# Two of three layer norms moved to ScalarE, a shorter output norm, and router weights written by GpSimd

## The chip, the cores and the metric
The kernel runs on one core of a Trainium2 chip. The metric is the time of one execution in microseconds. The core's engines work side by side, each through its own list of instructions: TensorE (PE in the rows, its weight loads PEld), VectorE (DVE), ScalarE (ACT), GpSimd (POOL) and SyncE (SP), which issues DMAs. They meet only at semaphores: an instruction may wait until a semaphore has reached a value, and everything behind it on its engine waits with it.

## What is computed
One decoder layer on x (8 batches x 512 tokens x 256 features, fp32), in three steps, each on a normalized copy of x and added to x:
```
x = x + attn(layernorm(x))       # gated slot attention: 4 heads, 64 slots, a recurrence over the tokens
x = x + xattn(layernorm(x))      # 16 heads against 64 context rows, softmax with 1 added to the denominator
x = x + moe(layernorm(x))        # 8 experts, top 2 of 8, 1280 places per expert, silu gate
layernorm(x) = (x - mean) / sqrt(var + 1e-5)
```
The slot attention ends in an output norm for each head, `o = o * rsqrt(mean(o*o) + 1e-5) * g_norm_w`, where o is a softmax-weighted sum, so that o is an unnormalized sum u divided by the softmax's denominator s. The router takes the two largest of 8 logits, gives them the weights 1/(1+e) and e/(1+e) with e = exp(second - first), and a token keeps its place with an expert only while that expert has taken fewer than 1280.

## The kernel before
The first stage goes over 32 chunks of 128 tokens, four to a batch. The second goes over the experts in 40 groups of 256 places.

Each engine's list for the chunk stage is written by hand as a `step` (PE L1516, DVE L1190, ACT L779, POOL L610): a fixed order of named pieces of work, each with a lag. `run(2, x_scores)` in step s means the piece for chunk s-2. So a step holds the slot attention of chunk s (lag 0) and its end for chunk s-1, the cross attention's start for s-1 and its middle for s-2, its end and the router's norm for s-3, and the routing for s-4. The first two batches and the last lagging steps are unrolled; the six batches between run in a loop, whose turn falls on the first chunk of a batch.

What the change and the prediction touch:
- **Norms.** `statistics` (L902) makes mean and variance on DVE in x_mv (r_mv, f_mv) and var+eps; `power` (L543) on POOL raises that to -0.5 (x_rstd, r_rstd, f_rstd); `norm` (L913) on DVE applies (x - mean) * rstd, giving f_xn, x_xn and r_xn. The norms are f (first), x (before the cross attention, lag 1) and r (before the router, lag 3). r_norm writes the row twice, 512 columns, into r_xn, whose rows are sent to the experts; each row has two more columns, the token's number and its weight.
- **Order on DVE** at the end of a step: residual2, start_states, r_statistics, residual1, x_statistics, causal_scores, x_norm, r_norm, slot_logits, gate_probs.
- **Order on POOL:** f_power, values, head_power, send_rows, keys (only a batch's first chunk, at lag 1: two 128x512 products, k_bd), r_power, hidden_keys (hid, from the mask), x_power. `hold` (L539) is a 128x1 add into idle_g that only takes time.
- **Order on ACT:** ..., o_columns, x_exp, ks_columns (k_z, s_z), e_columns (e_t, the copy of the cross attention's transposed exponentials), x_columns, softmax_exp (b_e), r_columns, p_columns, x_queries, squares.
- **Order on PE:** ..., scores, e_columns, logits, x_columns (transposes of x_xn and hid), values (the product of e_t with v_bd), r_columns, p_columns (transposes of b_p), x_queries, mix, sum_states, read_out.
- **Output norm:** DVE sums squares (b_ss), multiplies twice by the softmax's reciprocal (b_t1, b_t2), scales and adds eps (b_ms), POOL raises to -0.5 (b_rms), DVE multiplies by the reciprocal (b_w) and applies it (b_o). Between them DVE runs x_maximum (sc_m).
- **Routing:** top_two (L1136) ends in `both`, which PE counts; places (L1160) makes the place numbers, the weights r_p and r_p*r_e, writes them into r_xn, and ends in `send`, on which POOL's send_rows (L597) waits before it issues two indirect DMAs.

Of the kernel before, what the change touches and what calls it, by code (L numbers as in the profile page):

```python
# [70 lines left out]
ROUTE_STEPS = 11  # L71
# [5 lines left out]
def decoder_layer(nc, x, qpos, kpos, mask, ctx_t, wq, wk, wv, wf, gnorm, wo,  # L77
# [5 lines left out]
    with ctx:  # L83
# [9 lines left out]
        neg_half = sb("neg_half", [P, 4])  # L93
        idle_v, idle_g = sb("idle_v", [P, 1]), sb("idle_g", [P, 3])
# [24 lines left out]
        def part1(name, shape, dt=F32):  # L119
# [49 lines left out]
        lg_m, b_sum, b_rec, b_ss, b_t1, b_t2, b_ms, b_rms, b_w = (  # L169
            part1(t, [P, H]) for t in ("lg_m", "b_sum", "b_rec", "b_ss", "b_t1", "b_t2", "b_ms", "b_rms", "b_w"))  # L170
# [7 lines left out]
        x_st, x_mv, x_var, x_rstd = (part1(t, [P, w]) for t, w in (("x_st", 6), ("x_mv", 2), ("x_var", 1), ("x_rstd", 1)))  # L178
        x_xn = part1("x_xn", [P, D])
# [23 lines left out]
        base = part1("base", [P, 2])  # L203
# [41 lines left out]
        def sems(names):  # L245
# [9 lines left out]
        logits_mm, lg_ok, lgm_ok, lgd_ok, be_ok, bsum_ok, brec_ok, bp_ok, p_mm, p_ok, mix_mm, mix_ok = sems(  # L255
            "logits_mm lg_ok lgm_ok lgd_ok be_ok bsum_ok brec_ok bp_ok p_mm p_ok mix_mm mix_ok")
        read_mm, sq_ok, rms_step, ms_ok, rms_ok, bw_ok, bo_ok, o_mm, o_ok, y_mm, x1_ok = sems(
            "read_mm sq_ok rms_step ms_ok rms_ok bw_ok bo_ok o_mm o_ok y_mm x1_ok")
# [82 lines left out]
        CONSTS = 19 + XH  # L341
# [138 lines left out]
        def _(pool):  # L480
# [10 lines left out]
            pool.memset(neg_half[:, :], -0.5).then_inc(consts_step, 1)  # L491
            pool.memset(taken[:, :], 0.0).then_inc(consts_step, 1)
# [4 lines left out]
            pool.wait_ge(consts_step, 7 + XH)  # L497
# [13 lines left out]
            pool.wait_ge(consts_step, 13 + XH)  # L511
# [11 lines left out]
            pool.wait_ge(consts_step, 18 + XH)  # L523
# [123 lines left out]
        def _(act):  # L647
# [47 lines left out]

            def e_columns(n, c, b):
# [63 lines left out]
            def squares(n, c, b):  # L760
                act.wait_ge(read_mm, n + 1)
                if later(n, 1):
                    act.wait_ge(rms_step, 3 * n)
# [9 lines left out]
            def router_exp(n, c, b):  # L773
                act.wait_ge(gap_ok, n + 1)
                if later(n, 1):
                    act.wait_ge(slots_ok, n)
                act.activation(r_e[:, :], gap[:, :], ACT.Exp).then_inc(re_ok, 1)

            def step(run):  # L779
# [9 lines left out]
                run(0, ks_columns)  # L789
                run(2, e_columns)  # L790
# [55 lines left out]
        def _(dve):  # L846
# [176 lines left out]
            def softmax_sum(n, c, b):  # L1023
# [3 lines left out]
                dve.reciprocal(b_rec[:, :], b_sum[:, :]).then_inc(brec_ok, 1)  # L1027
# [8 lines left out]
            def head_squares(n, c, b):  # L1036

                dve.wait_ge(sq_ok, n + 1)
                dve.tensor_reduce(b_ss[:, :], b_sq[:, :, :], AX.X, ALU.add).then_inc(rms_step, 1)
                dve.wait_ge(rms_step, 3 * n + 1)  # L1040
                dve.wait_ge(brec_ok, n + 1)
                dve.tensor_tensor(b_t1[:, :], b_ss[:, :], b_rec[:, :], ALU.mult).then_inc(rms_step, 1)

            def head_squares2(n, c, b):
                dve.wait_ge(rms_step, 3 * n + 2)
                dve.tensor_tensor(b_t2[:, :], b_t1[:, :], b_rec[:, :], ALU.mult).then_inc(rms_step, 1)
                dve.wait_ge(rms_step, 3 * n + 3)
                if later(n, 1):
                    dve.wait_ge(rms_ok, n)
                dve.tensor_scalar(b_ms[:, :], b_t2[:, :], 1.0 / M, EPS, ALU.mult, ALU.add).then_inc(ms_ok, 1)  # L1050

# [569 lines left out]
```

## Time and profile before
| | |
|---|---|
| runs | 1523.87, 1531.29, 1534.08 us (median 1531.29) |
| the profiled execution | 1525.26 us, its span 1523.5 us |
| PE busy | 1406.5 us (92%) |
| PE weight loads | 1257.8 us (83%) |
| DVE busy | 952.5 us (63%) |
| ACT busy | 657.0 us (43%) |
| POOL busy | 351.9 us (23%) |
| mean granted clock of PE | 0.967 |

A busy share is the part of the span in which an engine executed instructions; matmuls are pipelined and their ends are modelled, so a busy PE isn't PE at its peak. The shares are averages over two stages of different kinds. In a timeline row stand the start, the busy time (both us), the engine, the line, the operation and its tiles; in square brackets, where there is one, the idle time of the engine just before it and what ended that. Rows of one line are merged where they follow each other.

### The profile page before, as it was taken

Reading aid. Unit: us, or ns where it says so; the run is one execution under the profiler, and the core shown is the slowest. Engines: PE = TensorE matmul, PEld = TensorE weight load, DVE = VectorE, ACT = ScalarE, POOL = GpSimd, SP = SyncE. Lnnn points to the kernel's source line nnn. Section 1 sums busy time; section 2 is a strip of 40 time slices with the busy share of each in tenths; the row PEclk is TensorE's granted clock in tenths of the full one; section 3 lists DMA queues with packets and bytes.
Section 4 is the critical chain, followed back from the end, with each engine's and each line's share of the span. In section 5 each row is a group of like instructions: output and inputs, shape, how many; then the busy total and the mean of one; then the engine's idle time right before and its main releaser. Section 6 shows DMA issues by size and latency. Waiting matters only on the chain. (4 is left out here: it accounts for less than half of the span.)

```text
span 1523.5 us, 31744 instructions
## 1 busy us (share of the span) xinstructions
PE 1406.5 (92%) x10457; PEld 1257.8 (83%) x10457; DVE 952.5 (63%) x3165; ACT 657.0 (43%) x1658; POOL 351.9 (23%) x523
## 2 busy tenths in 40 slices
PE   5699999999999999999975999999999999999995
PEld 3577777777777777777754999999999999999995
DVE  4367787787787787777744555556554555556442
ACT  1244554454554554454413444334443444344331
POOL 3112322232231322322212112122111212122122
PEclk8799999999999999999966999999999999999998
DMA  9300010010100100000006133142414133142111
GB/s 278 102 12 17 31 31 16 31 30 15 30 30 15 30 30 16 30 30 15 22 21 210 26 81 63 29 117 34 115 29 113 31 74 78 29 122 33 29 22 22
DMA packets 67288, 79.62 MB, mean 52 GB/s; under 512 B 11091, under 2 KB 60724, under 8 KB 67155
## 3 DMA queue, kind: packets, MB, share of 16 engines
q1 hardware_dynamic: 52562, 59.09, 12.8%
q0 software_dynamic: 14592, 18.91, 7.6%
q8 instruction: 65, 1.06, 0.3%
q14 instruction: 69, 0.56, 0.1%
HBM read 44.04 MB, written 33.96 MB: 51 GB/s over the span
## 5 line engine op out<-in xcount | busy, mean ns | idle before, releaser
L830 ACT ACTIVATE h_a<-banks 128x256 f32<-128x256 f32 x320 | 122.5, 383 | 359.2 <-PE banks L1309 359.2
L1241 DVE TENSOR_TENSOR h_f<-banks,h_a 128x256 f32<-128x256 f32 x320 | 135.7, 424 | 158.6 <-ACT h_a L830 149.0
L541 POOL TENSOR_TENSOR idle_g<-half 128x1 f32<-128x1 f32 x144 | 29.8, 207 | 709.5 <-DVE y_s L1260 409.6
L1309 PE MATMUL banks<-xe_t_hi,w_even_hi 128*128 128x256 f32 x640 | 180.2, 282 | 0.9 <-DVE h_f L1241 0.9
L1309 PE MATMUL banks<-xe_t_hi,w_odd_hi 128*128 128x256 f32 x640 | 179.5, 280 | 0.0
L1309 PE MATMUL banks<-xe_t_lo,w_even_hi 128*128 128x256 f32 x640 | 178.3, 279 | 0.0
L1309 PE MATMUL banks<-xe_t_hi,w_even_lo 128*128 128x256 f32 x640 | 178.2, 279 | 0.0
L1309 PE MATMUL banks<-xe_t_lo,w_odd_hi 128*128 128x256 f32 x640 | 177.9, 278 | 0.0
L1309 PE MATMUL banks<-xe_t_hi,w_odd_lo 128*128 128x256 f32 x640 | 177.8, 278 | 0.0
L817 ACT ACTIVATE h_t_hi<-h_f 128x256 fp32r<-128x256 f32 x320 | 131.8, 412 | 32.6 <-DVE h_f L1241 32.2
L1248 DVE TENSOR_TENSOR h_t_lo<-h_f,h_t_hi 128x256 fp32r<-128x256 f32 x320 | 133.8, 418 | 6.1 <-ACT h_t_hi L817 4.3
L635 POOL DMA_INDIRECT out_dram<-y_s,token x80 | 124.7, 1559 | 27.0 <-issue 19.9
L1309 PEld LDWEIGHTS banks<-xe_t_hi,w_even_hi 128*128 128x128 f32 x640 | 121.1, 189 | 1.1 <-DVE h_f L1241 1.1
L1309 PEld LDWEIGHTS banks<-xe_t_lo,w_even_hi 128*128 128x128 f32 x640 | 121.4, 190 | 0.0
L1309 PEld LDWEIGHTS banks<-xe_t_lo,w_odd_hi 128*128 128x128 f32 x640 | 121.0, 189 | 0.0
L1309 PEld LDWEIGHTS banks<-xe_t_hi,w_even_lo 128*128 128x128 f32 x640 | 120.8, 189 | 0.0
L1309 PEld LDWEIGHTS banks<-xe_t_hi,w_odd_hi 128*128 128x128 f32 x640 | 120.3, 188 | 0.0
L1309 PEld LDWEIGHTS banks<-xe_t_hi,w_odd_lo 128*128 128x128 f32 x640 | 120.1, 188 | 0.0
L1309 PE MATMUL banks<-w_in,f_xnt 128*128 128x512 f32 (+1 forms) x256 | 99.8, 513 | 1.9 <-ACT f_xnt L655 1.9
L1258 DVE CAST token<-about 128x1 uint32<-128x1 f32 x80 | 8.6, 149 | 134.0 <-PE banks L1309 134.0
L1309 PE MATMUL banks<-w_odd_hi,h_t_hi 128*128 128x256 f32 x320 | 88.8, 278 | 0.0
L1309 PE MATMUL banks<-w_even_hi,h_t_hi 128*128 128x256 f32 x320 | 88.8, 278 | 0.0
(240 smaller groups left out, 3669.3 us busy)
## 6 DMA issues: line engine op xcount, KB each, us to landing
raw<-in_w SPq DMA_DIRECT2D x24, 1024.0 KB, 8.3
expert_rows<-empty SPq DMA_DIRECT2D x4, 2580.0 KB, 22.4
xe<-expert_rows SPq DMA_DIRECT2D x40, 258.0 KB, 2.9
xin<-in_x SPq DMA_DIRECT2D x32, 128.0 KB, 2.2
out_dram<-x SPq DMA_DIRECT2D x32, 128.0 KB, 1.8
out_dram<-y_s,token POOLq DMA_INDIRECT x80, 3.8
mask_i<-in_mask SPq DMA_DIRECT2D x32, 32.0 KB, 1.8
expert_rows<-r_xn,send POOLq DMA_INDIRECT x64, 3.2
```

What stands on the lines that cost most here:

```text
L541: return pool.tensor_tensor(idle_g[:, i:i + 1], half[:, 0:1], half[:, 0:1], ALU.add)
L635: pool.indirect_dma_start(out=out, out_offset=bass.IndirectOffsetOnAxis(ap=token[par][a][:, :], axis=0), in_=y_s[:, par, a, :], in_offset= ...
L817: act.activation(h_t[0][:, par, f, :], h_f[:, f % 2, :], ACT.Copy).then_inc(h_hi_ok, 1)
L830: act.activation(h_a[:, f % 2, :], bank[2 + f % 4][:, 0:GS], ACT.Silu).then_inc(silu_ok, 1)
L1241: dve.tensor_tensor(h_f[:, f % 2, :], bank[2 + f % 4][:, GS:2 * GS], h_a[:, f % 2, :], ALU.mult)\
L1248: dve.tensor_tensor(h_t[1][:, par, f, :], h_f[:, f % 2, :], h_t[0][:, par, f, :], ALU.subtract)\
L1258: dve.tensor_copy(token[par][a][:, :], about[:, par, a, 0:1])
L1309: last = pe.matmul(dst, lhs, rhs, start=(i == 0), stop=(i == len(pairs) - 1))
```

## The change
Three edits, all in the chunk stage:
1. x_norm and r_norm are applied by ACT as scale*x + bias with scale rstd and bias -mean*rstd. POOL makes the bias (x_shift, r_shift) right after the power. On ACT the two stand between ks_columns and e_columns. f_norm stays on DVE.
2. The output norm's weight is one power: with s the softmax's sum, (ss/64 + eps*s*s)^-0.5 is the weight. The reciprocal, b_t1, b_t2 and b_w's product go; one scalar_tensor_tensor on s (b_floor) comes.
3. The router's weights and the token's number are written into r_xn by POOL in send_rows, the reciprocal as a power of -1. DVE's places gets shorter, hot is made by one instruction, and DVE's last routing step waits for the sends of two chunks before.

```
@@ gpsimd @@
+            def shift(n, mv, rstd, to, rstded, shifted, i):
+                pool.wait_ge(rstded, n + 1)
+                hold(i)
+                pool.tensor_scalar(to[:, :], mv[:, 0:1], rstd[:, 0:1], -1.0, ALU.mult, ALU.mult).then_inc(shifted, 1)
             def x_power(n, c, b):
                 power(n, x_var, x_rstd, x_vared, x_rstded, x_normed)
+                shift(n, x_mv, x_rstd, x_shift, x_rstded, x_shifted, 3)
             def r_power(n, c, b):
                 power(n, r_var, r_rstd, r_vared, r_rstded, r_normed)
+                shift(n, r_mv, r_rstd, r_shift, r_rstded, r_shifted, 4)
             def head_power(n, c, b):
-                power(n, b_ms, b_rms, ms_ok, rms_ok, bw_ok)
+                power(n, b_ms, b_w, ms_ok, bw_ok, bo_ok)
...
+                pool.wait_ge(re_ok, n + 1)
+                hold(0)
+                pool.tensor_scalar(r_den[:, :], r_e[:, :], 1.0, 1e-12, ALU.add, ALU.add).then_inc(send_step, 1)
+                pool.wait_ge(send_step, n * SEND_STEPS + 1)
+                pool.tensor_tensor(r_p[:, :], r_den[:, :], neg_one[:, :], ALU.pow).then_inc(send_step, 1)
+                pool.tensor_copy(r_xn[:, par, :, D:D + 1],
+                                 token_no[:, bass.ds(n, 1)].rearrange("p (a b) -> p a b", b=1).to_broadcast([P, 2, 1]))
+                pool.wait_ge(send_step, n * SEND_STEPS + 2)
+                pool.tensor_tensor(r_xn[:, par, 1, D + 1:ROW], r_p[:, :], r_e[:, :], ALU.mult)
+                pool.tensor_copy(r_xn[:, par, 0, D + 1:ROW], r_p[:, :]).then_inc(send_step, 1)
                 pool.wait_ge(slots_ok, n + 1)
-                hold(0)
+                pool.wait_ge(r_normed, n + 1)
+                pool.wait_ge(send_step, n * SEND_STEPS + SEND_STEPS)
+                hold(5)
@@ scalar @@
+            def x_norm(n, c, b):
+                act.wait_ge(x_shifted, n + 1)
...
+                act.activation(x_xn[:, :], x1[:, c % 2, :], ACT.Identity, bias=x_shift[:, 0:1], scale=x_rstd[:, 0:1])\
+                   .then_inc(x_normed, 1)
+            def r_norm(n, c, b):
...
+                act.wait_ge(r_shifted, n + 1)
+                act.activation(r_xn[:, c % 2, :, 0:D],
+                               x2[:, c % 2, :].rearrange("p (a d) -> p a d", a=1).to_broadcast([P, 2, D]),
+                               ACT.Identity, bias=r_shift[:, 0:1], scale=r_rstd[:, 0:1]).then_inc(r_normed, 1)
...
                 run(0, ks_columns)
+                run(3, r_norm)
+                run(1, x_norm)
                 run(2, e_columns)
@@ vector @@
-                dve.reciprocal(b_rec[:, :], b_sum[:, :]).then_inc(brec_ok, 1)
+                dve.scalar_tensor_tensor(out=b_floor[:, :], in0=b_sum[:, :], scalar=EPS, in1=b_sum[:, :],
+                                         op0=ALU.mult, op1=ALU.mult).then_inc(floor_ok, 1)
...
-                dve.tensor_tensor(b_t1[:, :], b_ss[:, :], b_rec[:, :], ALU.mult).then_inc(rms_step, 1)
...
-                dve.tensor_tensor(b_t2[:, :], b_t1[:, :], b_rec[:, :], ALU.mult).then_inc(rms_step, 1)
...
-                dve.tensor_scalar(b_ms[:, :], b_t2[:, :], 1.0 / M, EPS, ALU.mult, ALU.add).then_inc(ms_ok, 1)
+                dve.scalar_tensor_tensor(out=b_ms[:, :], in0=b_ss[:, :], scalar=1.0 / M, in1=b_floor[:, :],
+                                         op0=ALU.mult, op1=ALU.add).then_inc(ms_ok, 1)
...
-                dve.tensor_tensor(b_w[:, :], b_rms[:, :], b_rec[:, :], ALU.mult).then_inc(bw_ok, 1)
...
-                for k in range(2):
-                    dve.tensor_scalar(hot[:, k, :], expert_no[:, :], top_f[:, k:k + 1], None, ALU.is_equal)\
+                dve.tensor_tensor(hot[:, :, :], expert_no[:, :].rearrange("p (a e) -> p a e", a=1).to_broadcast([P, 2, E]),
+                                  top_f[:, :].rearrange("p (k a) -> p k a", a=1).to_broadcast([P, 2, E]), ALU.is_equal)\
...
-                dve.tensor_scalar(base[:, :], top_f[:, :], float(CAP), None, ALU.mult).then_inc(route_step, 1)
-                dve.wait_ge(re_ok, n + 1)
-                dve.tensor_scalar(r_den[:, :], r_e[:, :], 1.0, 1e-12, ALU.add, ALU.add).then_inc(route_step, 1)
...
-                dve.reciprocal(r_p[:, :], r_den[:, :]).then_inc(route_step, 1)
...
-                dve.tensor_tensor(slot_f[:, :], pos[:, :], base[:, :], ALU.add).then_inc(route_step, 1)
...
-                dve.tensor_copy(r_xn[:, c % 2, 0, D + 1:ROW], r_p[:, :])
-                dve.tensor_tensor(r_xn[:, c % 2, 1, D + 1:ROW], r_p[:, :], r_e[:, :], ALU.mult)
+                dve.scalar_tensor_tensor(out=slot_f[:, :], in0=top_f[:, :], scalar=float(CAP), in1=pos[:, :],
+                                         op0=ALU.mult, op1=ALU.add).then_inc(route_step, 1)
...
-                run(1, x_norm)
-                run(3, r_norm)
```

## Rows read from the trace of the kernel before
**Rows 1.** Busy time by stretch: PE, PEld, DVE, ACT, POOL, clock, DMA share, GB/s.
```profile
400.00:500.00 100.00, 92.96 (x607) 74.34 (x606) 79.46 (x316) 52.88 (x134) 28.20 (x45) 1.00 0.09 26
...
820.00:1500.00 680.00, 675.86 (x5867) 675.09 (x5866) 362.79 (x914) 283.89 (x723) 134.34 (x152) 1.00 0.28 63
```
**Rows 2.** Waits, 100 to 740 us: who waited for whom, us in total, times, longest.
```profile
PE banks L1309 <- DVE both L1158: 5.7, 5, 1.2
...
PE banks L1309 <- DVE g_s L946: 5.0, 24, 0.2
PE banks L1303 <- DVE f_xn L915: 4.0, 5, 0.9
...
PE banks L1303 <- DVE b_p L1020: 1.7, 7, 0.2
```
**Rows 3.** Timeline of a batch's third step: start, us, engine, line, operation, idle before.
```profile
447.49 0.19 ACT L777 ACTIVATE r_e<-gap 128x1 f32<-128x1 f32 x1
...
449.45 0.19 POOL L541 TENSOR_TENSOR idle_g<-half 128x1 f32<-128x1 f32 x1 [4.97 <-DVE send L1188]
...
452.88 1.16 PE L1309 MATMUL banks<-q_t,k_z 128*128 128x128 f32 x8 [0.33 <-issue]
...
453.43 0.56 POOL L548 TENSOR_TENSOR r_rstd<-r_var,neg_half 128x1 f32<-128x1 f32 x1 [0.84 <-DVE r_var L911]
...
453.98 0.18 POOL L541 TENSOR_TENSOR idle_g<-half 128x1 f32<-128x1 f32 x1
454.13 0.44 POOL L594 TENSOR_SCALAR hid<-mask_i 128x64 f32<-128x64 int32 x1
...
454.75 0.57 POOL L548 TENSOR_TENSOR x_rstd<-x_var,neg_half 128x1 f32<-128x1 f32 x1 [0.18 <-DVE x_var L911]
455.01 1.08 ACT L701 ACTIVATE e_t<-banks 128x512 f32<-128x512 f32 x2 [1.39 <-PE banks L1477]
...
455.43 0.41 DVE L915 TENSOR_SCALAR x_xn<-x,x_mv,x_rstd 128x256 f32<-128x256 f32 x1 [0.21 <-POOL x_rstd L548]
...
456.44 0.39 PE L1303 MATMUL banks<-ident,x_xn 128*128 128x128 f32 x2
...
456.66 1.86 PEld L1309 LDWEIGHTS banks<-v_bd,e_t 128*128 128x128 f32 x16
...
459.01 0.20 PEld L1303 LDWEIGHTS banks<-ident,b_p 128*128 128x128 f32 x2 [0.35 <-DVE b_p L1020]
```
**Rows 4.** Groups of POOL's instructions, 0 to 60 us: count, busy us, mean ns.
```profile
L530 POOL TENSOR_SCALAR sl<-slopes 128x16 f32<-128x16 f32 x1 | 1.1, 1107 | 0.1
```
**Rows 5.** Groups of ACT's instructions, 0 to 740 us.
```profile
L716 ACT ACTIVATE f_e<-f_abs 128x256 f32<-128x256 f32 x31 | 12.9, 417 | 0.0
...
L648 ACT ACT_TABLE_LOAD x1 | 1.3, 1283 | 0.8 <-PEq L1612 0.8
```
**Rows 6.** Timeline of a batch's second step, with k_bd.
```profile
429.82 2.05 POOL L570 TENSOR_TENSOR k_bd<-k_all,diag 128x512 f32<-128x512 f32 x2
...
434.36 1.86 PEld L1309 LDWEIGHTS banks<-v_bd,e_t 128*128 128x128 f32 x16
...
436.84 0.44 PE L1303 MATMUL banks<-ident,b_p 128*128 128x128 f32 x2 [0.24 <-DVE b_p L1020]
```
**Rows 7.** Timeline of a batch's first step, in two batches.
```profile
402.99 0.20 ACT L777 ACTIVATE r_e<-gap 128x1 f32<-128x1 f32 x1 [0.78 <-DVE gap L1147]
...
403.88 0.18 PE L1309 MATMUL banks<-both,before 128*128 128x8 bf16 x1 [1.15 <-DVE both L1158]
...
409.78 0.58 POOL L548 TENSOR_TENSOR x_rstd<-x_var,neg_half 128x1 f32<-128x1 f32 x1
...
411.72 1.86 PEld L1309 LDWEIGHTS banks<-v_bd,e_t 128*128 128x128 f32 x16
...
489.51 0.16 DVE L1042 TENSOR_TENSOR b_t<-b_ss,b_rec 128x4 f32<-128x4 f32 x1
489.70 0.16 DVE L1046 TENSOR_TENSOR b_t<-b_t,b_rec 128x4 f32<-128x4 f32 x1
```

More of the change, by code:

```diff
@@ L70 @@
 SPARE = B * T
-ROUTE_STEPS = 11
+ROUTE_STEPS = 7
+SEND_STEPS = 3
 PIECES = 6
@@ L168, in decoder_layer @@
         lg, lg_d, b_e = (part1(t, [P, H, M]) for t in ("lg", "lg_d", "b_e"))
-        lg_m, b_sum, b_rec, b_ss, b_t1, b_t2, b_ms, b_rms, b_w = (
-            part1(t, [P, H]) for t in ("lg_m", "b_sum", "b_rec", "b_ss", "b_t1", "b_t2", "b_ms", "b_rms", "b_w"))
+        lg_m, b_sum, b_floor, b_ss, b_ms, b_w = (
+            part1(t, [P, H]) for t in ("lg_m", "b_sum", "b_floor", "b_ss", "b_ms", "b_w"))
         b_p = part1("b_p", [P, D])
@@ L178, in decoder_layer @@
         x_st, x_mv, x_var, x_rstd = (part1(t, [P, w]) for t, w in (("x_st", 6), ("x_mv", 2), ("x_var", 1), ("x_rstd", 1)))
+        x_shift, r_shift = part1("x_shift", [P, 1]), part1("r_shift", [P, 1])
         x_xn = part1("x_xn", [P, D])
@@ L339, in is_last @@
             return isinstance(n, int) and n == last
-        CONSTS = 19 + XH
+        CONSTS = 20 + XH
         W_LOADS = 11 + B
@@ L694, in ks_columns @@
                     last.then_inc(done, 1)
+            def x_norm(n, c, b):
+                act.wait_ge(x_shifted, n + 1)
+                if later(n, 1):
+                    act.wait_ge(x_cols_mm, n)
+                act.activation(x_xn[:, :], x1[:, c % 2, :], ACT.Identity, bias=x_shift[:, 0:1], scale=x_rstd[:, 0:1])\
+                   .then_inc(x_normed, 1)
+            def r_norm(n, c, b):
+                if later(n, 2):
+                    for k in range(2):
+                        act.wait_ge(sent[2 * (c % 2) + k], (n - c % 2) * 8)
+                    act.wait_ge(r_cols_mm, n - 1)
+                act.wait_ge(r_shifted, n + 1)
+                act.activation(r_xn[:, c % 2, :, 0:D],
+                               x2[:, c % 2, :].rearrange("p (a d) -> p a d", a=1).to_broadcast([P, 2, D]),
+                               ACT.Identity, bias=r_shift[:, 0:1], scale=r_rstd[:, 0:1]).then_inc(r_normed, 1)
             def e_columns(n, c, b):
@@ L1071, in x_statistics @@
                 statistics(n, x1[:, c % 2, :], x_st, x_mv, x_var, x_stats, x_vared, x_rstded)
-            def x_norm(n, c, b):
-                if later(n, 1):
-                    dve.wait_ge(x_cols_mm, n)
-                norm(n, x1[:, c % 2, :], x_xn[:, :], x_mv, x_rstd, x_rstded, x_normed)
             def x_maximum(n, c, b):
@@ L1118, in r_statistics @@
                 statistics(n, x2[:, c % 2, :], r_st, r_mv, r_var, r_stats, r_vared, r_rstded)
-            def sent_before(n, c):
-                if later(n, 2):
-                    for k in range(2):
-                        dve.wait_ge(sent[2 * (c % 2) + k], (n - c % 2) * 8)
-            def r_norm(n, c, b):
-                sent_before(n, c)
-                if later(n, 2):
-                    dve.wait_ge(r_cols_mm, n - 1)
-                norm(n, x2[:, c % 2, :].rearrange("p (a d) -> p a d", a=1).to_broadcast([P, 2, D]),
-                     r_xn[:, c % 2, :, 0:D], r_mv, r_rstd, r_rstded, r_normed)
-                dve.tensor_copy(r_xn[:, c % 2, :, D:D + 1],
-                                token_no[:, bass.ds(n, 1)].rearrange("p (a b) -> p a b", b=1).to_broadcast([P, 2, 1]))
             def top_two(n, c, b):
@@ L1151, in top_two @@
                 dve.wait_ge(route_step, n * ROUTE_STEPS + 2)
[L1152 to L1155 removed]
+                dve.tensor_tensor(hot[:, :, :], expert_no[:, :].rearrange("p (a e) -> p a e", a=1).to_broadcast([P, 2, E]),
+                                  top_f[:, :].rearrange("p (k a) -> p k a", a=1).to_broadcast([P, 2, E]), ALU.is_equal)\
+                   .then_inc(route_step, 1)
+                dve.wait_ge(route_step, n * ROUTE_STEPS + 3)
                 if later(n, 1):
@@ L1194, in step @@
                 run(1, head_squares)
-                run(1, head_squares2)
                 run(2, x_maximum)
-                run(1, head_weights)
                 run(1, head_outputs)
```

53 lines of the change are left out of this document (23 added, 30 removed).

## The prediction
> **What bounds the kernel now.** The stretches by engine come first [rows 1]. The stretch from 400 to 500 us stands for the stage of the 32 chunks: TensorE (PE) is busy 93 us of 100 there, VectorE (DVE) 79, ScalarE (ACT) 53, GpSimd (POOL) 28. From 820 us the experts run, PE busy 676 of 680 us; the change touches nothing there. So whatever the change is worth, it is worth it in the chunk stage, and only where PE waits.
>
> The waits of that stage come next [rows 2]. PE's idle time that ends on a DVE result is small: 5.7 us before the counts, 5.0 before the gate sums, 4.0 before the transposes of f_xn, 1.7 before those of b_p, together 16.4 us of 640. That is the most that a lighter DVE can give back, and DVE's 79% is no bound.
>
> Then the timeline of one ordinary chunk, row by row [rows 3]. PE takes its work in the written order: logits, transposes of x_xn (456.44), values (456.77). The values product reads e_t, which ACT begins at 455.01 and ends at 456.09, before PE comes to it. The transposes need x_xn, which DVE ends at 455.84 (455.43 and 0.41), also before. Both have about 0.5 us of slack and no more. In front of x_xn stands POOL's chain: r_rstd 453.43, hold, hid 454.13, x_rstd 454.75 to 455.32, nearly without a gap. POOL is mostly idle over a chunk, but not in these two microseconds.
>
> **The change, part by part.** Times are those of the chunk in [rows 3] unless said otherwise.
>
> *Shift chain on POOL.* The two norms become scale and bias on ACT, so POOL must also make -mean*rstd. Behind r_rstd come a wait for it, a hold and a 128x1 tensor_scalar; the same behind x_rstd. A hold passes in 0.15 (453.98 to 454.13). No row shows a warm 128x1 tensor_scalar: from below it is bounded by the 128x1 add, 0.19 busy; from above by hid, 128x64, 0.44; far above lies the setup's first one, 1.1 us [rows 4]. I take 0.30, between the two warm ones, and 0.07 for a wait on POOL itself (between 0 and 0.15). So each shift adds 0.52. r_rstd ends at 453.99, r_shift at 454.51, hid (0.15 and 0.44) at 455.10, x_rstd (0.57) at 455.67, x_shift at 456.19.
>
> *Norms on ACT.* They stand behind ks_columns and ahead of e_columns. ACT's 256 columns from SBUF take 0.417 [rows 5]; DVE took 0.41 for x_xn. r_norm (512 columns, at most twice that) waits for r_shift and runs from 454.6 to 455.4, covered. x_norm waits for x_shift: 456.29 to 456.71. Behind it on ACT waits e_columns, whose input has been ready since 455.01; it now runs from about 456.67 to 457.75 (1.08 in all). So PE comes to x_xn's transposes 0.3 late, and to the values product at 457.8 instead of 456.7 (weight load): **1.1 us later**. What follows on PE (the b_p transposes, which waited 0.35 for their weights, [rows 3], some 0.1 of it on PE) is then ready, which gives back 0.1. Net 1.0. All later work of the chunk hangs on PE's order, so none of this is made up.
>
> The Trainium skill ("ScalarE: Activation LUTs", Rules for kernel authors) says to put multiply and add on VectorE, which it gives as up to about 3 times faster than ScalarE in bf16. The rows show 0.41 against 0.417 for this fp32 size, so the trace does not bear it out. By the rule's factor x_norm would take 1.2 us and each chunk 0.8 us more, 26 us in all.
>
> *Router weights on POOL.* DVE sheds base, r_den, r_p, two writes to r_xn and the token column; POOL gains a hold, a tensor_scalar, a power of one column (0.57, as x_rstd), two copies and a product (0.2 each, as the hold), and a second hold. They can start when r_e is there (447.68) and end by 449.4. The first hold before the sends stood at 449.45, released by DVE's send, which comes some 0.2 earlier now: the sends move by nothing. With 0.44 per tensor_scalar and 0.3 per small one they would be 0.55 late. What hides that is POOL's wait of 0.84 ahead of r_rstd [rows 3], except where k_bd is built.
>
> *Chunk with keys.* In one chunk of four POOL builds k_bd (2.05) between the sends and r_rstd [rows 6], from 429.82 to 431.87, so there is no gap for the shifts to fall into. With the steps above r_rstd ends at 432.44, r_shift at 432.96, hid at 433.55, x_rstd at 434.12, x_shift at 434.64, x_norm at 435.15, e_t at 436.2, and values starts 1.8 later than its 434.36 (weight load). PE's wait of 0.24 for b_p goes. Net 1.6.
>
> *First chunk of a batch.* The loop's turn makes DVE late, and PE waits 1.15 for both [rows 7]. Here the lighter DVE counts: two b_t steps, b_w and one hot go ahead of it, at 0.19 each (from 489.51 to 489.70 for the first), so both comes 0.75 earlier, r_e some 0.5 earlier (ACT waited 0.78 for gap), and the sends 0.7 earlier. POOL ran its chain here without a gap, so x_rstd moves from 409.78 to 409.6 (0.7 earlier, 0.52 of r_shift later), x_shift ends at 410.7, x_norm at 411.2, e_t at 412.25; values starts 0.6 later than its 411.72, less the 0.1 of b_p. Net 0.5.
>
> *Output norm by one power.* The reciprocal becomes a scalar_tensor_tensor of the same size; b_t twice and b_w leave DVE. Elsewhere than in the first chunk of a batch, sc_m behind them waits for PE and starts when it did, so 0.2 is gained at b_w and 0.17 at hot; g_s comes 0.24 earlier, and PE's wait of 0.2 before it closes. But the scores wait 0.33 behind k_z on ACT [rows 3], which hangs on qk_e, not on g_s, so the 0.2 reappears there. I cost it at nothing; if k_z were no wall it would give 0.2 x 24 = 5 us, the share of the g_s waits in [rows 2].
>
> **Sum.** A batch: 0.5 + 1.6 + 1.0 + 1.0 = 4.1 us, times 8 batches = 33 us. The profiled execution took 1525.3 us (span 1523.5); 1558 after. The three runs' median, 1531.3, lies 6 above it, so I put the median at 1561. With 0.19 for every tensor_scalar: about 3.0 a batch, 24 us, 1549. With 0.44 and slow copies: 0.8 + 2.4 + 1.3 + 1.3 = 5.8, 46 us, 1571 (median 1577).
>
> **Rivals.**
> (a) *The lighter DVE wins (faster).* Place: the counts and g_s waits. It decides if x_norm ends before about 455.55, so that e_t is not late. Then the 16.4 us of [rows 2] are open, at best 1515 by the median. Against it: x_rstd alone ended at 455.32 and two holds, two shifts and x_norm come on top, at least 1.2 us even with the add's price. 4%.
> (b) *The slip is absorbed.* PE comes late to values, but PE's records may hide idle time behind it (the ends of matmuls are modelled), or the delay may shrink later waits, such as the 0.33 a chunk before the scores; 18 us or more of the 33 would go, and 1546 or less would be left. For: these waits exist. Against: each of them hangs on work that starts after PE's own. 9%, of which 1% ends above the 15 us.
> (c) *POOL's tensor_scalar costs 1.1 us warm, as the setup's did* [rows 4]. Then POOL is late for the sends by 0.9 and each shift adds 1.3: some 2.6 to 4 us a chunk, 1610 to 1650. Against: hid, the same instruction on 64 columns, takes 0.44. 7%.
> (d) *Identity needs another activation table.* ACT loads a table once, 1.3 us [rows 5]; a switch before r_norm and one back before the softmax's exponential would add 2.6 us a chunk to an ACT that is now on the path: 33 + 83 us, 1647. For it: no Identity stands in the trace. Against: Copy, Square and Abs run beside Exp and Ln without a load. 2%.
> The Trainium skill ("ScalarE: Activation LUTs", Table sets) says that identity is in every set; by that rule (d) is void.
> (e) *The edits do nothing to the path* (all of it beside PE's work): 1531. That would need e_columns ahead of x_norm, which the diff excludes; it shares the chance of (b).
>
> **Numbers.** The forecast holds 78%. Predicted 1561. The range reaches from 1542 (below the cheapest prices, into (b)) to 1590 (above the dear ones, towards (c)). A measurement of this kernel can tell about 1% (15 us) from no change: faster 0.04, same 0.08, slower 0.88.
>
> **What would show it.** In the changed trace: ACT idle before x_xn with POOL x_shift as releaser, some 1 us in each chunk; ACT's idle time before e_t (1.39 in [rows 3]) gone; e_t beginning right behind x_xn; PE waiting for x_xn and e_t, 0.8 to 1.8 us a chunk together; DVE's share falling with PE no faster; PE's wait for both shrinking below 0.5. The forecast is wrong if PE does not wait for e_t, if the chunk stage lengthens by under 15 us, or if POOL's x_shift ends within 0.5 us of the old x_rstd.

## The result and the profile after
| | before | after |
|---|---|---|
| median | 1527.6 us (4 runs, 1523.87 to 1534.08) | 1646.57 us (4 runs, 1645.34 to 1650.31) |
| profiled execution, span | 1525.26, 1523.5 us | 1650.31, 1648.6 us |
| mean granted clock of PE | 0.967 | 0.919 |

After takes 1.0778 times as long [1.0729, 1.0827]: 119 us more, where 33 were forecast. (The four runs of before include the three of the table ahead of the prediction, whose median was 1531.29.)

The page of after: engines, and the granted clock in 40 slices (9 is 90% or more).
```profile
PE 1494.9 (91%) x10457; PEld 1342.5 (81%) x10457; DVE 899.7 (55%) x2781; ACT 693.4 (42%) x1722; POOL 427.5 (26%) x844
...
PEclk8799898999898998989887599999999999999998
```
Busy time by stretch of after, columns as in [rows 1]: the chunk stage, a pause and what follows it, the experts.
```profile
140.00:700.00 560.00, 509.09 (x2989) 418.42 (x2989) 341.94 (x1204) 267.73 (x660) 184.19 (x426) 0.90 0.07 23
...
485.00:489.70 4.70, 2.35 (x18) 1.76 (x16) 1.84 (x4) 2.53 (x5) 2.62 (x9) 1.00 0.03 7
489.70:499.00 9.30, 9.28 (x54) 9.28 (x55) 3.12 (x11) 1.83 (x6) 0.17 (x1) 0.63 0.00 0
...
940.00:1620.00 680.00, 677.81 (x5815) 677.62 (x5814) 360.72 (x908) 280.63 (x719) 134.80 (x152) 0.99 0.28 63
```
The same of before: the chunk stage, and the stretch behind a values product's start.
```profile
140.00:700.00 560.00, 529.07 (x3466) 424.87 (x3465) 435.63 (x1693) 281.16 (x715) 149.84 (x238) 1.00 0.08 25
...
456.50:466.00 9.50, 9.38 (x72) 7.90 (x72) 6.54 (x22) 2.60 (x8) 0.96 (x2) 1.00 0.00 1
```
The experts run as in [rows 1]. In the chunk stage DVE falls as meant, from 436 to 342 us of 560, and PE does less too: 2989 matmuls where there were 3466. The two rows in the middle hold the part that [rows 1] to [rows 7] do not show. PE is busy for 2.35 of 4.7 us and is granted 1.00; then it is busy for 9.28 of 9.30 us and is granted 0.63, a mixture of its two levels, 1.2 and 2.4 GHz. 54 matmuls pass there in 9.3 us, where before passed 72 in 9.5.

PE's waits of after, 100 to 860 us (who waited for whom, us in total, times, longest), to be held against [rows 2].
```profile
PE banks L1305 <- ACT x_xn L723: 22.1, 29, 1.7
PE banks L1311 <- ACT e_t L742: 16.9, 28, 0.8
...
PE banks L1305 <- ACT decay L788: 6.2, 24, 0.7
PE banks L1311 <- DVE both L1171: 4.2, 5, 0.9
...
PE banks L1311 <- DVE g_s L989: 1.1, 6, 0.2
```
The forecast waits are there, in every chunk: 39.0 us in about 28, of which 1.6 us (for x_xn, in the steps with k_bd) stood in before too. What the lighter DVE gives back is small. The wait for both falls from 5.7 to 4.2 us. The wait for g_s falls from 5.0 to 1.1, but the one for decay, which ACT makes from the product of g_s and which PE reads next but one, grows from 1.1 to 6.2: the 0.2 us a chunk is not gained, it is waited for one piece later. ACT's longer list is not the cause: norms_only below has that list and waits 1.1 us for decay from 100 to 740 us, and no_norms_pad has the short list and waits 5.1 us from 140 to 700. The timeline of a batch's second step, with k_bd, of after ([rows 6] of before):
```profile
485.83 0.26 POOL L560 TENSOR_SCALAR r_shift<-r_mv,r_rstd 128x1 f32<-128x1 f32 x1
...
486.74 0.56 POOL L551 TENSOR_TENSOR x_rstd<-x_var,neg_half 128x1 f32<-128x1 f32 x1
...
487.66 0.27 POOL L560 TENSOR_SCALAR x_shift<-x_mv,x_rstd 128x1 f32<-128x1 f32 x1
487.96 0.60 ACT L723 ACTIVATE x_xn<-x,x_shift,x_rstd 128x256 f32<-128x256 f32 x1 [0.94 <-POOL x_shift L560]
488.58 1.08 ACT L742 ACTIVATE e_t<-banks 128x512 f32<-128x512 f32 x2
488.61 0.44 PE L1305 MATMUL banks<-ident,x_xn 128*128 128x128 f32 x2 [1.65 <-ACT x_xn L723]
489.72 3.48 PE L1311 MATMUL banks<-v_bd,e_t 128*128 128x34 f32 x16 [0.56 <-ACT e_t L742]
```
And of an ordinary step, the third ([rows 3] of before):
```profile
513.32 0.57 POOL L551 TENSOR_TENSOR x_rstd<-x_var,neg_half 128x1 f32<-128x1 f32 x1
...
514.23 0.27 POOL L560 TENSOR_SCALAR x_shift<-x_mv,x_rstd 128x1 f32<-128x1 f32 x1
514.53 0.60 ACT L723 ACTIVATE x_xn<-x,x_shift,x_rstd 128x256 f32<-128x256 f32 x1 [0.94 <-POOL x_shift L560]
...
515.19 0.44 PE L1305 MATMUL banks<-ident,x_xn 128*128 128x128 f32 x2 [0.43 <-ACT x_xn L723]
516.48 2.93 PE L1311 MATMUL banks<-v_bd,e_t 128*128 128x34 f32 x16 [0.75 <-ACT e_t L742]
```
Three things are to be seen here. The order of the prediction is kept to the row: power, shift, x_norm, e_t, and PE at the end of it. PE pauses twice, 1.65 and 0.56 us in the second step, 0.43 and 0.75 in the third. And behind the pauses the same 16 matmuls of the values product last 3.48 and 2.93 us instead of 1.87.

How much that is, the groups of PE's matmuls tell: busy us and mean ns, first before (100 to 740 us), then after (100 to 860 us). Both stretches hold about 28 chunks.
```profile
L1309 PE MATMUL banks<-v_bd,e_t 128*128 128x34 f32 x448 | 52.4, 273 | 0.0
...
L1309 PE MATMUL banks<-x_xnt,xw 128*128 128x128 f32 x224 | 30.8, 282 | 0.0
L1309 PE MATMUL banks<-p_t,s_z 128*128 128x128 f32 x224 | 30.1, 278 | 0.0
...
L1477 PE MATMUL banks<-ident,ex 128*128 128x128 f32 x224 | 29.0, 273 | 0.0
```
```profile
L1311 PE MATMUL banks<-v_bd,e_t 128*128 128x34 f32 x448 | 75.5, 335 | 16.9 <-ACT e_t L742 16.9
...
L1311 PE MATMUL banks<-x_xnt,xw 128*128 128x128 f32 x231 | 53.1, 408 | 0.0
L1311 PE MATMUL banks<-p_t,s_z 128*128 128x128 f32 x232 | 48.3, 379 | 0.0
...
L1479 PE MATMUL banks<-ident,ex 128*128 128x128 f32 x232 | 30.1, 273 | 0.0
```
The transposes of ex stand ahead of the pauses and keep their 273 ns. The three products behind the pauses take 335, 408 and 379 ns instead of 273 to 282; for 28 chunks that is 23 + 21 + 16 = 60 us more, with no instruction added.

By the starts of the k_bd product one batch of four steps took 90.9 us before (23.77, 22.77, 22.17, 22.18) and takes 105.8 after (26.32, 27.80, 26.72, 24.95): 14.9 more, and 8 such batches make 119. The part of a step ahead of the values product grew by 1.15, 2.13, 1.56 and 1.36 us (6.2 a batch, some 50 us in 8): that is in the main the late x_xn and e_t, whose waits of 39.0 us in 28 chunks are 5.6 a batch. The part from there to the next k_bd product grew by 1.4, 2.9, 3.0 and 1.4 us (8.7 a batch, some 69 us in 8), and in that part PE waits for nothing new. It is granted less clock there:
```profile
489.72:499.23 9.51, 9.51 (x57) 9.51 (x57) 3.12 (x11) 1.81 (x6) 0.40 (x1) 0.64 0.00 0
...
543.01:550.90 7.89, 7.88 (x57) 7.88 (x57) 2.46 (x7) 1.82 (x6) 0.00 (x0) 0.78 0.00 1
```
The second part lasts 6.5 to 6.6 us at a clock of 1.00 (before), 7.9 at 0.78 and 9.5 at 0.64. Added up step by step over the 30 steps that both traces have in full, the first part grew by 46 us and the second by 62.

### The profile page after: what moved, and what is told of

Read it like the earlier page. It is cut to its first block and busy times, and to the rows that moved or that the text cites. A ratio compares the mean times of both kernels' runs of the same rounds, so it can differ in the third digit from the quotient of the medians.

```text
span 1648.6 us, 31758 instructions
## 1 busy us (share of the span) xinstructions
PE 1494.9 (91%) x10457; PEld 1342.5 (81%) x10457; DVE 899.7 (55%) x2781; ACT 693.4 (42%) x1722; POOL 427.5 (26%) x844
## 3 DMA queue, kind: packets, MB, share of 16 engines
q8 instruction: 65, 1.06, 0.3%
## 5 line engine op out<-in xcount | busy, mean ns | idle before, releaser
L544 POOL TENSOR_TENSOR idle_g<-half 128x1 f32<-128x1 f32 x240 | 48.4, 201 | 690.8 <-DVE y_s L1262 416.6
L551 POOL TENSOR_TENSOR f_rstd<-f_var,neg_half 128x1 f32<-128x1 f32 x32 | 17.6, 549 | 356.0 <-DVE f_var L954 356.0
L1311 PEld LDWEIGHTS banks<-v_bd,e_t 128*128 128x128 f32 x512 | 82.6, 253 | 30.4 <-ACT e_t L742 24.4
L1311 PE MATMUL banks<-v_bd,e_t 128*128 128x34 f32 x512 | 86.7, 336 | 21.7 <-ACT e_t L742 21.6
```

The costliest lines, as they stand in the source:

```text
L544: return pool.tensor_tensor(idle_g[:, i:i + 1], half[:, 0:1], half[:, 0:1], ALU.add)
L551: pool.tensor_tensor(rstd[:, :], var[:, :], neg_half[:, 0:var.shape[1]], ALU.pow).then_inc(done, 1)
L1311: last = pe.matmul(dst, lhs, rhs, start=(i == 0), stop=(i == len(pairs) - 1))
```

## The experiments
Times are medians. Each ratio stands against the kernel before, run on the same chip beside it (1521.8 to 1523.1 us). "Clock" and PE's waits are those of each kernel's trace from 140 to 700 us, the chunk stage; in that stretch before has 1.00, after 0.90. Amounts against after are differences of medians. After's ratio was measured beside a before of 1527.6 us; by the ratios these amounts are a few us smaller (59 us instead of 65 for filler, 51 instead of 59 for e_first, 108 instead of 111 for reordered).

| kernel | us | ratio [95%] | clock | PE waits there for x_xn; for e_t |
|---|---|---|---|---|
| norms_only | 1638.8 | 1.0793 [1.0734, 1.0852] | 0.90 | 17.3 in 22; 12.6 in 21 |
| no_norms | 1559.27 | 1.0248 [1.0204, 1.0293] | 0.96 | 2.6 in 6; none |
| e_first | 1587.26 | 1.0443 [1.0405, 1.0481] | 0.93 | 18.2 in 22; none |
| filler | 1581.65 | 1.0392 [1.0343, 1.0442] | 0.97 | 8.7 in 10; 7.5 in 19 |
| reordered | 1535.33 | 1.0071 [1.0042, 1.0101] | 0.99 | none |
| no_norms_pad | 1527.57 | 1.0029 [1.0003, 1.0055] | 0.99 | 2.6 in 6; none |
| late8 | 1584.14 | 1.0390 [1.0317, 1.0463] | 0.94 | 14.2 in 21; none |
| r_on_dve | 1616.39 | 1.0594 [1.0522, 1.0667] | 0.90 | 11.5 in 21; 12.7 in 22 |
| late8_fill | 1572.43 | 1.0324 [1.0263, 1.0385] | 0.96 | 9.8 in 22; none |
| late4 | 1536.42 | 1.0105 [1.0052, 1.0158] | 0.98 | 4.8 in 6; none |
| x_on_dve | 1545.24 | 1.0163 [1.0109, 1.0218] | 0.98 | 7.2 in 6; none |
| best | 1527.99 | 1.0027 [1.0002, 1.0053] | 0.99 | none |

**Which edit costs it.** norms_only is before with the first edit alone.
```
 before
+ shift behind x_power and r_power (POOL); x_norm and r_norm on ACT between ks_columns and e_columns
- x_norm, r_norm on DVE
  (output norm and router weights as before)
```


> The kernel before with the first edit alone: x_norm and r_norm on ScalarE behind ks_columns, their shifts on GpSimd; the output norm and the router's weights as they were. Theory A (the whole loss comes from x_norm standing behind GpSimd's shift chain and ahead of e_t: TensorE waits for x_xn and e_t, some 6.3 us a batch, and then works at a lower granted clock, some 8.7 us a batch): all of the 119 us, 1635 to 1655 us, clock about 0.92. Rival B (the router's weights on GpSimd or the shorter output norm carry a good part): under 1615 us.

Its 1638.8 us are 116 above before, inside the expected range: the first edit alone has the whole loss, with the waits of after and its clock of 0.90. Of edits 2 and 3 nothing is needed to explain after.

no_norms is the other half: after with both norms back on DVE and without shifts.
```
-                shift(...)                # behind x_power and r_power
-                run(3, r_norm)            # ACT
-                run(1, x_norm)
                 run(0, causal_scores)     # DVE
+                run(1, x_norm)
+                run(3, r_norm)
```


> The changed kernel with both norms back on VectorE and without shifts: the second and third edits alone. Theory A: no new wait of TensorE, the counts' wait in a batch's first step falls from 1.15 to about 0.4 us; 8 times 0.6 us is gained: 1518 to 1530 us, clock 0.967. Rival B (the router's weights cost time on GpSimd ahead of r_rstd): over 1545 us.

The expectation failed: this should have been close to before and was 37 us slower. Most of the loss has a place of its own, the loop's turn on DVE:
```profile
502.31 0.43 DVE L925 BATCH_NORM_STATS2 f_st<-xin 128x6 f32<-128x256 f32 x1 [3.40 <-issue]
504.53 0.18 DVE L928 BATCH_NORM_AGGREGATE f_mv<-f_st 128x2 f32<-128x6 f32 x1 [1.67 <-issue]
...
506.03 0.69 PE L1298 MATMUL banks<-ident,f_xn 128*128 128x128 f32 x2 [3.53 <-DVE f_xn L936]
```
DVE stands for 3.40 and again for 1.67 us with nothing in the profile that it waits for (in other turns up to 3.6 and 1.8), and PE then waits 3.53 us for f_xn (18.1 us in 5 turns; 4.0 in [rows 2]). The queue that carries instructions moves at such a turn, with packets of 8 KB each; first before (390 to 400 us), then no_norms (400 to 412 us), queue and kind, packets, MB, share of 16 engines:
```profile
q14 instruction: 2, 0.02, 0.5%
...
q14 instruction: 4, 0.03, 0.9%
```
One of before's two starts inside DVE's stall (393.3 to 395.9 us); of no_norms' four, two start inside the first stall (403.1 to 406.4) and one inside the second (407.0 to 408.8). Whether this belongs to what edits 2 and 3 compute, or to where the loop lies in DVE's list, is what the next kernel asks: no_norms with 24 one-column memsets ahead of the loop, which nobody reads.
```
+            for i in range(24):
+                dve.memset(pad_v[:, i:i + 1], 0.0)
             over_chunks(dve, step)
```


> The second and third edits alone, with 24 one-column memsets ahead of VectorE's chunk loop that nothing reads: the same loop at another place in VectorE's program. Theory E (the 37 us of the second and third edits alone are VectorE's fetch stall at the loop's turn, which depends on where the loop lies: 3.4 and 1.7 us there against 2.4 before): the stall is back to about 2.4 us and the time to 1520 to 1540 us. Rival F (the edits themselves cost it, by their work on GpSimd or the order of their waits): within 6 us of 1559.

1527.57 us, as expected: 32 us are gone with instructions added, and the second stall with them. So the stall comes and goes with where the loop lies, not with edits 2 and 3, and those cost 0.3% [0.03%, 0.55%] once it is away. In after the second stall does not appear; no term of its 119 us is due to it. The turns of no_norms_pad have two of these packets again (386 to 398 us). So the stalls stand beside fetched instructions, as the expectation supposed; that DVE waits for just these packets no row shows, nor why the place decides how many there are. The prediction's step for the first chunk holds here: PE's wait for both fell from 5.7 us in 5 to 2.3 in 5.

**The pause, or what follows it.** filler is after with work for PE ahead of its two waits: four transposes of the identity ahead of x_xn, two ahead of e_t, into PSUM columns that nobody reads.
```
             def x_columns(n, c, b):
+                bank_left(pe, "x_cols", n)
+                fill(tile["x_cols"][:, 3 * P:4 * P], 4)
                 pe.wait_ge(x_normed, n + 1)
             def values(n, c, b):
+                bank_left(pe, "values", n)
+                fill(tile["values"][:, 3 * P:4 * P], 2)
                 pe.wait_ge(et_ok, n + 1)
```


> The changed kernel with transposes of the identity into unused PSUM columns, four ahead of the wait for x_xn and two ahead of the wait for e_t, 1.5 us of TensorE's work a step that nothing reads. Theory A with the clock as the larger part: TensorE does not pause, the clock stays where it was before the change (0.967), and the time falls although work is added: to 1570 to 1590 us (1528 and 6.3 us a batch of waiting, and up to 10 us of overshoot). Rival D (the slower matmuls behind the wait come from something else, such as contention with GpSimd and ScalarE): clock unchanged at 0.92 and 1646 us or more.

PE has more to do, x_xn and e_t come no sooner, and 65 us are gone: 1581.65 us, in the expected range. The timeline of filler, an ordinary step and the one with k_bd two steps on:
```profile
505.87 0.44 PE L1305 MATMUL banks<-ident,x_xn 128*128 128x128 f32 x2
506.98 1.97 PE L1311 MATMUL banks<-v_bd,e_t 128*128 128x34 f32 x16 [0.34 <-ACT e_t L742]
...
555.36 0.61 PE L1305 MATMUL banks<-ident,x_xn 128*128 128x128 f32 x2 [1.23 <-ACT x_xn L723]
556.47 3.63 PE L1311 MATMUL banks<-v_bd,e_t 128*128 128x34 f32 x16
```
Where the pause that is left is 0.34 us the values product takes 1.97 us; where it is 1.23 us it takes 3.63 here. (Two of seven steps with k_bd kept the full clock behind such a pause, those at 356.91 and 753.05.) The ordinary steps take 23.3 and 23.5 us (24.9 and 26.7 in after, 22.2 before); those with k_bd 24.6 to 28.9.

This shows the second cost apart from the first. Over the same 30 steps as above, against before, the two parts of a step grew by:

| kernel | ahead of the values product | behind its start |
|---|---|---|
| after | 46 us | 62 us |
| norms_only | 47 us | 67 us |
| filler | 47 us | 6 us |
| e_first | 25 us | 30 us |
| late8 | 21 us | 34 us |
| r_on_dve | 37 us | 60 us |

In filler the chain is as late as in after, within 1 us, and what was lost behind the pause has come back, 56 of 62 us.

late8 makes the pause without ACT: before, with a wait and eight holds on POOL ahead of x_rstd. All norms stay on DVE.
```
             def x_power(n, c, b):
+                pool.wait_ge(x_vared, n + 1)
+                for i in range(8):
+                    hold(3 + i)
                 power(n, x_var, x_rstd, x_vared, x_rstded, x_normed)
```


> The kernel before, with eight holds on GpSimd ahead of each x_rstd, behind a wait for x_var: nothing else differs, and x_xn comes 1.2 us later. Theory A: TensorE pauses 0.6 us more in three steps of a batch and 1.2 more where k_bd is built: 24 us of waiting, 1547 us if the clock holds, and 1560 to 1590 us if the pauses cost clock too. Rival B (the holds are hidden): 1522 us.

A late x_xn is enough: 61 us more, as expected, clock 0.94, with ACT's list as before. Two of its steps:
```profile
429.23 0.44 PE L1306 MATMUL banks<-ident,x_xn 128*128 128x128 f32 x2 [0.43 <-DVE x_xn L918]
429.62 1.87 PE L1312 MATMUL banks<-v_bd,e_t 128*128 128x34 f32 x16
...
453.13 0.44 PE L1306 MATMUL banks<-ident,x_xn 128*128 128x128 f32 x2 [1.38 <-DVE x_xn L918]
453.52 2.53 PE L1312 MATMUL banks<-v_bd,e_t 128*128 128x34 f32 x16
```
A pause of 0.43 us left the rate alone here, one of 1.38 did not. The length alone doesn't decide: a pause of 0.39 us at 478.82 stood in a step of 24.5 us, of which others with the same pause took 22.9 (22.2 in before). There the values product still ran at its old pace (1.87 us) and the two products behind it took 1.90 and 1.89 us instead of 1.06.

late4 is the same with four holds.
```
+                pool.wait_ge(x_vared, n + 1)
+                for i in range(4):
+                    hold(3 + i)
```


> The kernel before with four holds ahead of x_rstd instead of eight: x_xn comes 0.6 us later, which the slack of 0.5 us takes up in three steps of a batch; where k_bd is built TensorE pauses 0.6 us more. Theory A: 5 us of pauses and up to 1.5 us of clock in each of 8 such steps: 1528 to 1542 us. If a shorter chain cost in proportion to the eight holds, it would be 1553 us.

15 us more, as expected. Waits for x_xn are left only in the steps with k_bd (4.8 us in 6), and nearly all that was lost is there: two of seven take 23.3 us and five take 24.6 to 26.1, where before took 22.8. The pause is 0.8 us in all seven, so the same pause was followed by the lower clock in some steps and not in others.

late8_fill is late8 with two transposes of the identity ahead of PE's wait for x_xn.
```
             def x_columns(n, c, b):
+                bank_left(pe, "x_cols", n)
+                for _ in range(2):
+                    pe.transpose(tile["x_cols"][:, 3 * P:4 * P], ident[:, :], ident[:, :])
                 pe.wait_ge(x_normed, n + 1)
```


> The kernel before with the eight holds ahead of x_rstd (1584 us alone), and two transposes of the identity into unused PSUM columns on TensorE ahead of the wait for x_xn, 0.5 us a step that nothing reads. Theory A (35 of the 61 us of the holds are the lower clock behind the pause): in the steps without k_bd TensorE hardly pauses, the clock is back near 0.96 and the time falls to 1550 to 1565 us. Rival D (the pause costs its own length and nothing else, the rest is something in the holds): 1584 us or more.

12 us back, of 61, and the 1550 to 1565 us that were expected are missed: the intervals of the two kernels overlap. The direction is filler's, the amount small: two transposes leave 9.8 us of the waits in 22 steps, up to 1.2 us long.

**The order on ACT.** e_first is after with e_t's copy ahead of the norms, and r_norm moved behind softmax_exp.
```
-                run(3, r_norm)
-                run(1, x_norm)
                 run(2, e_columns)
+                run(1, x_norm)
                 run(1, x_columns)
                 run(0, softmax_exp)
+                run(3, r_norm)
```


> The changed kernel with another order on ScalarE: e_columns ahead of the norms, r_norm behind softmax_exp. Theory A: e_t is in time again and only the wait for x_xn is left, 0.4 to 1.7 us a step; if the clock falls by the whole idle time, it falls less: 1570 to 1620 us. Rival C (ScalarE's longer list itself is the bound, 0.60 and 0.81 us for the two norms, wherever they stand): within 15 us of 1646.

The wait for e_t is gone and 59 us with it, as expected; the wait for x_xn is as in after (18.2 us in 22 steps; 15.9 in 21 there). Half of the loss comes from e_t's copy, ready long before, standing behind the norms.

reordered goes further: the same order of e_columns and x_norm, softmax_exp ahead of x_columns, and on PE the values product ahead of x_xn's transposes, so that 1.9 us of work lie between e_t and x_xn.
```
@@ scalar @@
-                run(3, r_norm)
-                run(1, x_norm)
                 run(2, e_columns)
-                run(1, x_columns)
+                run(1, x_norm)
+                run(3, r_norm)
                 run(0, softmax_exp)
+                run(1, x_columns)
@@ tensor @@
-                run(1, x_columns)
                 run(2, values)
+                run(1, x_columns)
```


> The changed kernel in another order: on ScalarE e_columns, x_norm, r_norm, softmax_exp, x_columns; on TensorE the values product ahead of the transposes of x_xn. Same work. Theory A (all of the loss is TensorE's pauses and the clock after them): e_t is there when TensorE comes to values, and x_xn has 1.9 us more time, so no pause is left in steps 1, 3 and 4 and at most 0.2 us where k_bd is built: 1515 to 1535 us, clock 0.96 or more. Rival C (ScalarE's and GpSimd's longer lists are the bound): over 1580 us.

1535.33 us (0.3 above the expected range) with all three edits in it: 111 of the 119 us are gone and the clock stands at 0.99. This also rules out that ACT's and POOL's longer lists are the bound, since both are as long as in after. x_xn is as late as in after; PE just doesn't come to it sooner. Against before it is still slower by 0.7% [0.42, 1.01].

**Which of the two norms.** r_on_dve is after with r_norm alone back on DVE.
```
-                shift(n, r_mv, ..., 4)        # POOL
-                run(3, r_norm)                # ACT
+                run(3, r_norm)                # DVE, behind causal_scores
```


> The changed kernel with r_norm back on VectorE and without r_shift: only x_norm is on ScalarE. Theory A: x_shift ends 0.65 us earlier in each step, so the pauses before x_xn and e_t shrink from 0.8 a step each to about 0.4, and with shorter pauses the clock falls less: 1560 to 1600 us. Rival C (ScalarE's longer list is the bound): 0.81 us less a step, 1620 us.

The expectation failed: 1616.39 us, not 1560 to 1600. The wait for x_xn shrank (11.5 us in 21 steps; 15.9 in after) but the one for e_t did not (12.7 in 22; 12.6), and the clock stayed at 0.90: behind the start of the values product nearly as much is lost as in after, 60 of 62 us (table above). So shorter pauses were not followed by less of the lower clock. The 1620 us of rival C come near the measured time, but reordered has ACT's whole list and takes 1535 us, so it is not its reason.

x_on_dve is after with x_norm alone back.
```
-                shift(n, x_mv, ..., 3)        # POOL
-                run(1, x_norm)                # ACT
+                run(1, x_norm)                # DVE, behind causal_scores
```


> The changed kernel with x_norm back on VectorE and without x_shift: only r_norm is on ScalarE, ahead of e_columns. Theory A: r_shift still delays x_rstd by 0.6 us, about the slack of x_xn, and r_norm (0.81 us, from r_shift on) ends near 455.5, so e_t is 0.4 to 0.5 late and just in time: 1525 to 1550 us. If r_norm on ScalarE carried half the loss: 1585 us.

This one met its expectation. With x_norm alone on ACT 5.9% of the 7.8% remain, with r_norm alone 1.6%. In x_on_dve:
```profile
408.94 0.44 PE L1302 MATMUL banks<-ident,x_xn 128*128 128x128 f32 x2
...
432.28 0.44 PE L1302 MATMUL banks<-ident,x_xn 128*128 128x128 f32 x2 [1.26 <-DVE x_xn L949]
```
r_norm itself is covered, as predicted, but its shift on POOL holds x_rstd up in the step with k_bd: 24.97 us instead of 22.76 there, in six of seven batches (23.1 in the other, with a pause of 0.94 us), and 22.18 as before in the last step.

**A version that wins?** no_norms_pad has the lighter DVE without the late x_xn. best adds reordered's order to it.
```
@@ scalar @@
-                run(1, x_columns)
                 run(0, softmax_exp)
+                run(1, x_columns)
@@ tensor @@
-                run(1, x_columns)
                 run(2, values)
+                run(1, x_columns)
```


> The second and third edits alone with the 24 memsets ahead of VectorE's loop, and two exchanges of order: on TensorE the values product ahead of the transposes of x_xn, on ScalarE softmax_exp ahead of x_columns. Theory A: the 0.2 to 0.4 us pause before x_xn where k_bd is built goes, and with it the lower clock that follows it in some of these steps (1.5 us): 1508 to 1520 us. If the later x_xn transposes hold up x_queries instead: 1528 us or more.

1527.99 us, not 1508 to 1520: the expectation failed, and no version beats the kernel before. What takes the gain in the step with k_bd, in best:
```profile
433.17 0.42 PE L1301 MATMUL banks<-ident,x_xn 128*128 128x128 f32 x2
...
434.69 0.46 PE L1301 MATMUL banks<-ident,b_p 128*128 128x128 f32 x2 [0.78 <-DVE b_p L1042]
434.96 1.89 PE L1307 MATMUL banks<-x_xnt,xw 128*128 128x128 f32 x8
```
The wait for x_xn has become one for b_p, 0.78 us, and behind it x_queries runs at 1.89 instead of 1.06 us. The first step of a batch is 0.5 us shorter than before's, but three of seven steps with k_bd take 24.4 to 24.5 us instead of 22.9 (one of seven in before).

## Why the prediction was wrong
**Right:** the sign, the chain, and its order. ACT waits for x_shift, e_t starts right behind x_norm, PE waits for x_xn and e_t in every chunk, DVE is relieved and PE is no faster for it. POOL's pieces cost what was written: the 128x1 tensor_scalar 0.26 to 0.27 (0.30 taken), the shift chain from x_rstd's start to x_shift's end 1.18 us (1.09). The router's weights on POOL cost nothing that shows (norms_only without them is within 0.5% of after). The output norm was rightly put at nothing: the 0.2 us at g_s reappears, though at decay, not at k_z as the prediction had it. The first step's gain at both came in no_norms_pad (5.7 to 2.3 us in 5); in after it was smaller (4.2 in 5, the longest 0.9 us, where below 0.5 was forecast).

**Mis-sized, in the sum as it stood.** The prediction had the values product start 0.6, 1.8, 1.1 and 1.1 us later in the four steps of a batch (net of small gains 4.1 in all). The part of a step ahead of it grew by 1.15, 2.13, 1.56 and 1.36, 6.2 in all: some 50 us in 8 batches, not 33. The chain explains most of that. x_norm took 0.60 us, not 0.417, since [rows 5] shows an activation whose scale and bias are constants and x_norm's are read from tiles; with the 0.1 at POOL that is some 0.3 a step. In the first step PE's wait for both fell by 0.3 us, not 0.75. PE's waits for x_xn and e_t together are 1.18 us in the ordinary step shown, inside the 0.8 to 1.8 of the prediction, and 2.21 with k_bd, outside. Two slips in the prediction change little: its own terms, 1558 and the 6 us by which the median lies higher, make 1564, not 1561; and the 16.4 us leave out 1.6 us that PE waited for x_xn in the steps with k_bd (PE, L1303, 7 times), where there was no slack at all. The groups of ACT's instructions, after:
```profile
L733 ACT ACTIVATE r_xn<-x,r_shift,r_rstd 128x512 f32<-128x512 f32 x22 | 17.9, 815 | 28.3 <-POOL r_shift L560 28.3
L723 ACT ACTIVATE x_xn<-x,x_shift,x_rstd 128x256 f32<-128x256 f32 x22 | 13.2, 600 | 20.7 <-POOL x_shift L560 20.7
L757 ACT ACTIVATE f_e<-f_abs 128x256 f32<-128x256 f32 x21 | 8.8, 418 | 0.0
```
600 less 418 is 182 ns for the two operands. The Trainium skill ("ScalarE: Activation LUTs", What ACT_TABLE_LOAD costs) gives about 93 ns for each such operand, 186 for two, which this trace bears out. With it the 0.417 of the prediction becomes an estimate of 0.60.

**The step that failed:** "Net 1.0. All later work of the chunk hangs on PE's order, so none of this is made up." It took the work behind PE's wait at the length that it had in a trace without such a wait. It has another: 8.7 us a batch, some 69 of the 119 us, are matmuls behind the pause at the lower granted clock. The prediction nowhere speaks of the clock; the sum had no term for it and no rival did, although each pause in it was priced. The runs bear it out from four sides: PE given other work in the pause (filler, 65 us back with the chain as late), a pause made by other means (late8, 61 us with the norms on DVE), the order changed so that no pause before x_xn or e_t is left (reordered, 111 us back with every edit kept), and the group of matmuls ahead of the pause, which kept its 273 ns.

Could it have been seen beforehand? The trace of before has rows for either answer: the stretch behind a loop turn with PE's longest pause [rows 7], the stretch behind the transposes of x_xn in one step with k_bd, and the chunk stage's last 120 us, where the steps thin out.
```profile
403.90:418.30 14.40, 13.72 (x107) 12.43 (x108) 11.09 (x46) 8.10 (x20) 4.46 (x8) 1.00 0.14 39
...
342.00:350.20 8.20, 7.95 (x59) 7.72 (x57) 4.29 (x16) 2.11 (x6) 0.41 (x1) 0.79 0.00 0
...
700.00:820.00 120.00, 88.31 (x507) 70.12 (x508) 76.60 (x306) 43.42 (x100) 32.13 (x46) 0.80 0.16 54
```
Behind a pause of 1.15 us the clock stayed at 1.00. Behind one of 0.23 us (before x_xn, at 341.62) it was 0.79, once in seven batches, and that step took 24.3 us instead of 22.8. A stretch with many pauses was granted 0.80. The first row alone would have spoken for the prediction's sum. The other two say that the granted clock can fall in this kernel's chunk stage, and that a forecast which puts a pause into every chunk needs a term for it, or at least a rival.

**The rivals.** (a) and (b) fell: nothing was won or absorbed. (c) fell, at 0.26 us for the tensor_scalar, not 1.1. (d) fell: ACT loads its table once up to 900 us of after, Identity or not. Its 1647 us are the measured number by accident. The Trainium skill's rule that identity is in every table set ("ScalarE: Activation LUTs", Table sets) agrees with this trace for the one set that it uses. (e) came up in an unforeseen form: with e_columns ahead and PE's order changed (reordered) the edits do come to almost nothing, 0.7%.

**Open.** Which pauses are followed by the lower clock. Seven steps with k_bd of each trace are counted here: how long PE paused before x_xn's transposes, and in how many of the seven the part behind the values product's start was granted less than 0.9 of the clock.

| kernel | pause before x_xn, us | lower clock behind it, of 7 |
|---|---|---|
| before | 0.2 | 1 |
| no_norms_pad | 0.4 | 4 |
| late4 | 0.8 | 5 |
| filler | 1.2 | 5 |
| x_on_dve | 1.3 (0.9 once) | 6 (not behind the 0.9) |
| late8 | 1.3 to 1.4 | 7 |
| after | 1.6 to 1.7 | 7 |

The longer pause is followed by it more often, but the same pause is not always followed by it, and the runs don't show what decides. Nor do they show why the loop's place in DVE's list decides how many packets of instructions come at its turn, and whether they are the stall.

## What to carry to other kernels
A pause of about a microsecond on a TensorE that is otherwise kept busy can cost itself and then the work behind it: here some 50 us of delay brought some 69 us of slower matmuls. So a change that makes PE wait where it did not is to be priced with its surroundings at the lower clock as well; and the first repair is the order on the feeding engine and on PE (what is ready goes first), not a faster producer. Before an operation moves to another engine, look at what stands behind it there: with e_t's copy ahead of the norms half of the loss was gone.

## What the runs showed of the hardware that was not expected
- Unread matmuls in a pause made the kernel faster by 65 us (filler against after).
- The same pause of 0.8 us was followed by a lower granted clock in five of seven steps and not in two (late4).
- Activations with scale and bias from tiles: 600 ns for 256 columns, 815 for 512; with constants 418 for 256.
- At the loop's turn DVE stood 2.6 us at most before its first instruction in before (12.1 us in 5 turns), and up to 3.6 and 1.8 us in no_norms. 24 memsets ahead of the loop moved it back (12.1 in 5), worth 32 us. Packets on the instruction queue stand beside the stalls: two at a turn in before, four in no_norms.
